# A hyperbolic-attention and fp8 layer: a new way to the first attention step, in one block

## The reference

```
arg    = max(1 + 2c |q - k|^2 / max((1 - c|q|^2)(1 - c|k|^2), EPS), 1 + EPS)
scores = -softplus(beta) * arccosh(arg) / sqrt(c) - attention_bias
w      = softmax(scores);   out = w @ log_map(v);   x1 = x + log_map(exp_map(out)) @ W_o^T
out    = x1 + bf16(fp8(LayerNorm(x1)) @ fp8(W_ffn) * scales) + bias
```

## Time and profile before

| | us |
|---|---|
| median of 3 runs | 2226.95 |
| lowest, highest | 2209.66, 2231.99 |
| the profiled execution's own time | 2226.39 |
| its span, first to last instruction | 2224.1 |

### The profile page before, as it was taken

One profiled execution on the slowest core, in us unless ns is written; L12 is line 12 of the kernel. 1 busy time (PEld: TensorE's weight loads), 2 busy tenths in 40 slices (PEclk: granted clock), 3 DMA queues, 4 the chain that ended last, 5 costly groups with the idle time before them and its releaser, 6 DMA issues. The chain is left out here.

```text
span 2224.1 us, 29561 instructions
## 1 busy us (share of the span) xinstructions
PE 1855.3 (83%) x10721; PEld 617.0 (28%) x10721; DVE 1172.3 (53%) x2869; ACT 1896.5 (85%) x1055; POOL 2.6 (0%) x15
## 2 busy tenths in 40 slices
PE   4459898998989859898989789898989898899792
PEld 2222222232322213222222222222222223233221
DVE  5563345555555545556555655555565555423335
ACT  1019999989999949999999699999999999999790
POOL 0000000000000000000000000000000000000000
PEclk9969999989999969999999899999999999999895
DMA  1031220313131211312213031312213031311000
GB/s 40 22 111 48 80 69 20 120 39 120 39 101 39 99 40 39 103 37 91 67 56 103 19 120 39 101 39 91 67 39 115 25 110 39 110 39 58 20 20 30
DMA packets 112937, 142.54 MB, mean 64 GB/s; under 512 B 35676, under 2 KB 61533, under 8 KB 112733
## 3 DMA queue, kind: packets, MB, share of 16 engines
q1 hardware_dynamic: 112732, 140.13, 20.1%
HBM read 85.07 MB, written 55.05 MB: 63 GB/s over the span
## 5 line engine op out<-in xcount | busy, mean ns | idle before, releaser
L888 ACT ACTIVATE U<-U,sc 128x2048 f32<-128x2048 f32 x512 | 1047.6, 2048 | 0.3
L881 ACT ACTIVATE U<-ps 128x2048 f32<-128x2048 f32 x500 | 959.8, 1920 | 63.6 <-PE ps L797 57.7
L797 PE MATMUL ps<-q_T,k_T 18*128 18x512 f32 x4096 | 638.8, 655 | 183.3 <-ACT U L881 132.7
L810 PE MATMUL ps<-U,vals 128*32 128x512 f32 x4096 | 564.9, 624 | 50.3 <-ACT U L888 42.6
L797 PEld LDWEIGHTS ps<-q_T,k_T 18*128 18x128 f32 x4096 | 200.4, 188 | 406.5 <-ACT U L881 318.1
L347 PE MATMUL ps<-wT,xnT 128*128 128x384 f32 x512 | 247.8, 574 | 17.1 <-DVE qkv L373 14.3
L373 DVE COPY qkv<-ps 128x384 f32<-128x384 f32 x128 | 71.3, 557 | 260.0 <-PE ps L347 259.9
L833 PE MATMUL ps<-woT,ident 128*128 128x256 f32 x428 | 157.9, 452 | 0.0
L956 DVE COPY OTs<-ps 128x512 f32<-128x512 f32 x64 | 44.3, 692 | 194.9 <-PE ps L810 173.4
L352 PE MATMUL ps<-ident,rows 128*128 128x128 f32 x512 | 110.3, 315 | 44.1 <-DVE rows L482 29.8
L347 PEld LDWEIGHTS ps<-wT,xnT 128*128 128x128 f32 x512 | 83.9, 202 | 222.9 <-issue 119.7
(11 more groups left out here) (164 smaller groups left out, 1168.9 us busy)
## 6 DMA issues: line engine op xcount, KB each, us to landing
rqb<-q_scratch SPq DMA_DIRECT2D x64, 1024.0 KB, 5.6
q_scratch<-q_T SPq DMA_DIRECT2D x16, 1024.0 KB, 4.5
k_scratch<-k_T SPq DMA_DIRECT2D x16, 1024.0 KB, 6.8
v_scratch<-vals SPq DMA_DIRECT2D x16, 768.0 KB, 9.2
xt<-in_L_attn_x_dram SPq DMA_DIRECT2D x16, 512.0 KB, 6.2
fi_xt<-in_L_attn_x_dram SPq DMA_DIRECT2D x16, 512.0 KB, 5.7
out_dram<-fi_x SPq DMA_DIRECT2D x16, 512.0 KB, 4.1
rk_scratch<-rk SPq DMA_DIRECT2D x16, 32.0 KB, 11.9
```

Of the source, the lines that this page charges most:

```text
L797: ins = pe.matmul(g.ps[:, 2 * pair + i, :], a.k_T[HB * h:HB * h + RD, b % 2, hg, kt * P:(kt + 1) * P], a.q_T[HB * h:HB * h + RD, G % 3, hg ...
L810: ins = pe.matmul(g.ps[HB * h:HB * h + VW, 6, :], a.vals[:, b % 2, kt, (hg * HPG + h) // 2, DH * (h % 2):DH * (h % 2) + VW], U[:, n % RING ...
L881: act.activation(U[:, n % RING].rearrange("p b n -> p (b n)"), chunk(n), ACT.Ln, scale=-2.0 / EPS, bias=1.0).then_inc(freed, 1)
L888: act.activation(U[:, n % RING], U[:, n % RING], ACT.Exp, scale=g.NEGB).then_inc(exp_done, 1)
```

## The change

The setup is no longer a block: `setup_stage` gives its pieces to the one block that is left, with its scratch in tiles that are used later (U, xb, sq and ocT of the finish stage). Every engine's order up to the first steps is written anew:

- SP issues x of group 0 first, then the weights, the scalars, x of group 1 (into the finish stage's xt), the FFN weight, and x of group 2.
- VectorE normalises group 0, computes the constants, normalises group 1, and then does each group's roots and rows (`first_vector`). Squares are done by ScalarE (`first_scalar`), sums by VectorE. The FFN weight is quantised in step 12.
- GpSimd clears and marks rows and vals (`pool_zero`).
- TensorE fills X, M and R of groups 0 and 1 in the order FIRST_FILLS, through banks 2 to 7; ScalarE empties them. The rows of k are formed and turned before those of q. A uses of group 0 have banks 0 and 1.
- distances(0) follow after R4 and R0 of group 0. The six other R of group 0 are filled after distances(1, 0), and copied by ScalarE in step 0. The R and A uses of group 1 lie in steps 2 to 20 (FIRST_USES), group 2's projection is wholly in the steps, with its own table (SECOND_USES). Group 1's stores are at step 21.

In the steps: the Exp's scale is a register, loaded once from g.NEGB; the small exponential e is in slot 20 instead of 19; on the open branch bound(n + 1) and clamp(n + 1) stand ahead of the copies of step n; copy_sums stands behind the copies of both halves; steps 0 to 2 hold no fillers.

```diff
+FIRST_USES = {("R", 4): (2, 0), ("A", 0): (2, 0), ("A", 1): (2, 1), ("R", 5): (3, BOTH), ("R", 6): (6, BOTH),
+              ("R", 7): (14, BOTH), ("R", 0): (16, BOTH), ("R", 1): (17, BOTH), ("R", 2): (19, BOTH),
+              ("R", 3): (20, BOTH)}
+SECOND_USES = dict(PROJECT_USES)
+SECOND_USES.update({("R", i): (24 + i, 0 if i in (3, 6) else BOTH) for i in range(8)})
+SECOND_USES.update({("A", 0): (27, 1), ("A", 1): (30, 1)})
+FIRST_FILLS = ([("X", 0, 0, 6), ("X", 0, 1, 7)] + [("M", 0, i, (2, 3, 4, 5, 6, 7, 2, 3)[i]) for i in range(8)]
+               + [("X", 1, 0, 4), ("X", 1, 1, 5)] + [("M", 1, i, (6, 7, 2, 3, 4, 5, 6, 7)[i]) for i in range(8)]
+               + [("R", 0, 4, 4), ("R", 0, 0, 5)]
+               + [("R", 0, i, bank) for i, bank in ((5, 6), (1, 7), (6, 6), (2, 7), (7, 6), (3, 7))])
...
+    def pool_zero(pool, setup):
+        step = Steps(pool, zeroed, 0)
+        step(pool.memset(rows[:, :, :, :, :], 0.0))
+        step(pool.memset(a.vals[:, :, :, :, DH:VW], 0.0))
+        step(pool.memset(rows[:, 0, :, :, 16:17], 1.0))
+        step(pool.memset(rows[:, 1, :, :, 17:18], -1.0))
+        setup.await_eab(pool)
+        for kt in range(KT):
+            for half in range(2):
+                ones = a.vals[half * 64:half * 64 + 64, :, kt, :, DH + 2 * kt + half]
+                step(pool.tensor_scalar(ones, ones, g.EAB[half * 64:half * 64 + 64], None, ALU.add))
...
+    def first_scalar(act, j):
+        kind, n, i, bank = FIRST_FILLS[j]
+        src = g.ps[:, bank, :]
+        act.wait_ge(p_filled, j + 1)
+        if kind == "X":
+            act.activation(xnT[:, i, :], src, ACT.Copy).then_inc(p_copied, 1)
+        elif kind == "M":
+            t, half = i // 2, i % 2
+            act.activation(qkv_of(n)[:, t, 24 * half:24 * (half + 1), :].rearrange("p h d -> p (h d)"),
+                           src[:, 0:384], ACT.Copy).then_inc(p_copied, 1)
+            if half == 1:
+                act.wait_ge(p_copied, j + 1)
+                if n == 1:
+                    act.wait_ge(reduced, t + 1)
+                act.activation(squares(t), qkv_of(n)[:, t].rearrange("p h d -> p (h d)"), ACT.Square).then_inc(squared, 1)
+        else:
+            qk, hg = i // HG, i % HG
+            dst = a.k_T[:, 0, hg, 0:GTOK] if qk else a.q_T[:, 0, hg, :]
+            act.activation(dst, src, ACT.Copy).then_inc(p_copied, 1)
...
     def scalar(act, n, k):
-        if k == 19:
+        if k == 20:
...
+                setup.scalar_weights(act)
+                first_copies("X", 0, range(2))
+                setup.scalar_constants(act)
+                first_copies("M", 0, range(8))
+                first_copies("X", 1, range(2))
+                first_copies("M", 1, range(2))
+                project.scalar(act, 0, 20)
+                first_copies("M", 1, range(2, 8))
+                setup.await_constants(act)
                 act.activation(past[:, :], g.NEGB, ACT.Exp, scale=math.log(2.0 * U_EXACT + 1.0)).then_inc(past_rdy, 1)
+                act.reg_load(exponent, g.NEGB[0:1, :].bitcast(I32))
+                first_copies("R", 0, (4, 0))
...
-                    act.activation(U[:, n % RING], U[:, n % RING], ACT.Exp, scale=g.NEGB).then_inc(exp_done, 1)
+                    act.activation(U[:, n % RING], U[:, n % RING], ACT.Exp, scale=exponent).then_inc(exp_done, 1)
...
+                        if not is_open and n == 0:
+                            other_copies()
+                        if not is_open and n == 1:
+                            project.scalar(act, 1, 20)
...
-                        if is_open:
-                            clamp(n)
-                            if n + 1 < n0 + UNIT:
-                                bound(n + 1)
+                        if is_open and n + 1 < n0 + UNIT:
+                            bound(n + 1)
+                            clamp(n + 1)
                         for key in in_step(G, s, 0):
                             copy(*key)
+                        for key in in_step(G, s, 1):
+                            copy(*key)
                         if n % KT == 0 and n >= KT:
                             copy_sums(n // KT - 1)
-                        for key in in_step(G, s, 1):
-                            copy(*key)
...
+                        if n == KERNEL_STEP:
+                            setup.vector_kernel(v)
...
+                for k in range(3):
+                    project.vector(v, 0, k, first)
+                setup.vector(v)
+                for k in range(3):
+                    project.vector(v, 1, k, first)
+                project.first_vector(v, 0, first)
+                for i in range(2):
+                    project.copy(v, 0, ("A", i))
+                project.first_vector(v, 1, first)
```

More of the change, by code:

```diff
@@ L366, in copy @@
         b, u = n // 2, n % 2
-        bank = g.ps[:, 7, :]
-        v.wait_ge(a.b7_filled, uses.after((kind, n, i)))
+        if n:
+            bank = g.ps[:, 7, :]
+            v.wait_ge(a.b7_filled, uses.after((kind, n, i)))
+        else:
+            bank = g.ps[:, i, :]
+            v.wait_ge(a_filled, i + 1)
         if kind == "X":
@@ L480, in vector @@
         if k == 23:
-            for qk in range(2):
+            for qk in (1, 0):
                 v.tensor_tensor(rows[:, qk, :, :, 0:DH], qkv[:, :, qk * H:(qk + 1) * H, :],
@@ L779, in _, with turned @@
                 sp.wait_ge(finish.stored, 16 * NG)
+            @block.gpsimd
+            def _(pool):
+                setup.pool_first(pool)
+                project.pool_zero(pool, setup)
             @block.tensor
             def _(pe):
+                def turned(n, i):
+                    if n == 0:
+                        pe.wait_ge(project.p_copied, FIRST_PLACE["R", n, i] + 1)
+                    else:
+                        pe.wait_ge(a.b7_copied, uses.after(("R", n, i)))
                 def distances(n, second):
@@ L871, in _, with first_copies, other_copies @@
                 act.preload_act_table_set(ACT_SET)
+                exponent = act.alloc_register("exponent")
+                def first_copies(kinds, n, numbers):
+                    for j, (kind, m, i, bank) in enumerate(FIRST_FILLS):
+                        if kind in kinds and m == n and i in numbers:
+                            project.first_scalar(act, j)
+                def other_copies():
+                    first_copies("R", 0, (1, 2, 3, 5, 6, 7))
                 def log(n, is_open):
@@ L924, in _ @@
             def _(v):
[L925 to L933 removed]
+                first = Steps(v, project.p_steps, 0)
+                first.mark(v.memset(ones_c[:, :], 1.0))
                 def bound(n):
@@ L1000, in unit @@
                             project.vector(v, m, k)
-                for k in range(LEAD):
-                    for half in range(2):
-                        for key in use_before_steps(k, half):
-                            copy(*key)
-                    for n, slot in before_steps(k):
-                        project.vector(v, n, slot)
+                        if n == KERNEL_STEP:
[9 more added lines that the diff above has]
+                project.first_vector(v, 1, first)
                 for n0 in range(0, N, UNIT):
```

450 lines of the change are left out of this document (260 added, 190 removed).

## The result

The changed kernel takes 2011.19 us (median of 4 runs, 2004.81 to 2014.07), the kernel before 2218.68 us beside it (4 runs, 2209.66 to 2231.99): a ratio of 0.9056 (0.8994 to 0.9119), 208 us less. The prediction of 2034.0 us is 23 us too high, and its range of 1995 to 2090 holds the time.

What follows compares the result with a forecast made beforehand. ScalarE was taken to bound the steps, with losses before the first step, at each projected group and on the open branch. Gains of 90 + 30 + 44 + 28 = 192 us from 2226.4 gave 2034 us, range 1995 to 2090.

Steps and rivals of the forecast that it cites:

- Part 1: Before the first step and in group 0: first Ln at 53 instead of 156 us; gain 90 us, bounds 70 to 98.
- two of them run at 2.93 us and six at 1.56 us: Group 0's eight M fills through six banks, without waiting for copies: two at half clock, six faster, ending at 31 us.
- at step 12 another 4 us of kernel quantisation: VectorE's quantisation before an M copy in group 0; with group 2's late normalisation, 6 us lost.
- Rival A: TensorE stays at half clock up to the first step: fourteen slower M fills, 19 us, so 2053 us; chance 0.15.
- Part 2: Exp's scale from a register saves 0.09 us each, 1.9 us a group, 30 us in all; bounds 0 to 60.
- Part 3: Small exponential one slot later: ScalarE's recurring wait for VectorE's nrm goes; gain 44 us, bounds 30 to 52.
- Part 4: Open branch: next step's bound and product go ahead of the bank-7 copy; gain 28 us, bounds 10 to 40.
- Part 5: The rest, including copy_sums behind its step's bank-7 copies: costed at nothing, or 20 us if the cover is gone.
- Rival C: TensorE, with VectorE's copies behind it, becomes the bound at 3.75 us an M step: 2077 us; chance 0.10.
- The rule on shared interfaces: GpSimd's tile clearing shares SBUF interfaces with VectorE, so VectorE's chain between 13 and 37 us would stretch; no size given.

Runs made afterwards that it cites:

- the yardstick: The changed kernel with no edit, run again as the reference of the experiments: 2010.25 us, ratio 0.9052 against the kernel before.
- the last experiment: Changed kernel with groups 1 and 2's uses kept out of group 0's steps 10 and 26, group 1's small exponential one step earlier: 2004.86 us, ratio 0.9025.

## Why the prediction was right, point by point

| part | forecast | measured | by |
|---|---|---|---|
| 1 way to the first step, group 0 included | 90 | 94.6; 81 to 99 | 107.5 - 12.9 in the two traces shown; between other pairs of executions |
| 2 register scale | 30 | 25 to 27 | alone in either kernel |
| 3 slot of e | 44 | 48 to 52; 51 | alone in the kernel before; groups 1 to 15 with it undone |
| 4 open branch | 28 | 40 | undone |
| 5 order of the sums | 0 | 6 to 8 | undone |
| whole | 192 | 208; 212; 221.1 | the medians; the medians beside the yardstick; the two spans shown |

Parts 2 to 5 close. Taken back one at a time, they lengthen groups 1 to 15 by 28.8, 50.9, 42.9 and 6.6 us in the traces, 129.2 in all, and between the kernel before and the changed kernel these groups differ by 125.7. Part 1 is weaker: it is only read off traces, no run had the old prologue with the new steps, and it depends on the execution. Up to the end of group 0 the three profiles with the old prologue take 271.5 to 285.6 us, and those of the changed kernel, of its second profile and of the experiment with the old open order 186.2 to 190.5: 81 to 99 us apart. The two executions shown are apart from their medians in opposite directions (2226.39 against 2218.68, 2004.81 against 2011.19), which is why 221.1 us lie between their spans and 208 between the medians. The forecast of 192 is 16 to 20 us below the medians, and these are the parts' own errors: parts 3 to 5 were sized some 25 us too small, part 2 some 4 too large. The luck is in part 1.

**Part 1** was right in the sum, as far as the executions let one tell, but from two errors that cancel. The first Ln came at 45.17 and not at 53. The step that failed is "two of them run at 2.93 us and six at 1.56 us": in this execution all eight ran fast, at 1.32 us each, and so shorter still than the 1.56 us of single fills with waits between them. M fills ended at 24.9 and not 31, nrm stood at 32.3 and not 37.5. Against it, the break before Ln(4) was larger than I had it: from Ln(0) to Ln(4) 26.1 us, where I had 23; that chain (copies, e of group 1, VectorE's second half, K rows, turn) was the right one, and the last experiment moved it. My other 6 us, "at step 12 another 4 us of kernel quantisation" and the late normalisation, had the right size and the wrong place: 6.2 us are lost in steps 10 and 26, where a second use meets the sums, and 2.6 us in step 4. That a moved table of uses puts new uses beside the sums can be read in the diff, and I didn't read it.

The granted clock can't decide at this place: it reads 1.00 up to 120 us in the kernel before, whose fills took 2.93 us from 35 to 64, and 1.00 in the changed kernel from 12 to 35 us, whose fills took 1.32. The durations tell the level. They are not the same in every execution: of ten profiles of kernels that keep this prologue, counting the moved clears and the single bank, five have the eight X products at 1.09 or 1.10 us and five at 1.97 us, and in the latter the first Ln of the unchanged prologue starts at 47.8 to 47.9 us, 2.7 us late. In these five the eight M fills take 12.8 to 13.1 us, so that the forecast's two slow fills are half right there (it had 15.3 us). Rival A, fourteen more slow fills, didn't come about in any. The prediction's remark that much of TensorE's busy time was at the half clock was too strong: the mean granted clock of the kernel before is 0.951, which is about a tenth of the span at the half clock, without the slow fills before the first step that this figure doesn't show.

**Part 2** was right in its mechanism: 1.9 us a group was forecast, 1.9 us measured in groups 1 to 13 of the changed kernel. The sum of 30 us is 3 to 5 us too large; group 0, where other waits rule, gave nothing visible.

**Part 3** was right in its mechanism, and 4 to 8 us small. With slot 20 alone, step 14 of groups 1 to 13 gave 40.7 us (38 forecast). Of the loss behind the stall I had counted 10 us out of 15; all of it went (14.9 us in steps 16 to 18). The W steps came to light and cost 6.6 us in step 15, where I had 4.

**Part 4** was right in its mechanism, and 12 us small. First to fourth Ln of the three units: forecast 21 us, 6 us saved, 14 us; measured 19.2, 7.1 saved (23.45 to 16.35), 13.3. That gives 33.9 us. What I left out are the steps behind the units: in group 5 the two distances of the Exps after them fell from 13.94 and 6.03 to 8.07 and 3.75 us.

**Part 5**: "I cost it at nothing" is the step that failed. The M copy that comes 0.6 us earlier was not hidden in the one step where it stands beside the sums, and that could be seen in the kernel before: 4.05 to 4.39 us among steps of 3.75.

**Rival C** was half there: M steps stay at 3.75 us and take 1 us a group from the register. The forecast had counted just that. **The rule on shared interfaces** did bite, by 2.3 us, of which all but the 0.24 us before the X fill were covered.

## What to carry to other kernels

Where an in-order engine waits for another for 2 us in a regular step, moving that one small instruction a step later can give back much more than the wait, since the next steps recover too; count everything up to the step at which the rhythm is even again. When a table of uses is moved, check each new place against what else the same engines do in that step, and look for steps a few tenths longer than their neighbours: they are where an order costs. A prologue is worth a timeline of its own, step by step with every engine, as it was nearly half of this gain. And where a clock has two levels, one profile of a prologue is one sample: here the first Exp came at 152.83 to 166.33 us with the same code before it, but for the small edits of the experiments.

## What the runs showed of the hardware that was not expected

A 4-element VectorE operation took 1.83 us instead of 0.17 while GpSimd cleared a tile, and ended 0.02 us after the clear. It is not every operation: the aggregate at 6.09 us, inside the same clear, took its usual 0.38 us. The Trainium skill, SBUF — State Buffer, section "SBUF: two separate sides", says that VectorE and GpSimd share a pair of ports as an exclusive lock, held for a whole instruction by whichever starts first, and that only some VectorE operations ask for it. The trace agrees, with 7.27 and 9.14 us as ends of the held operations beside 7.26 and 9.12 us of the clears.

The same code doesn't meet the same clock in every execution. In three profiles with the old prologue TensorE had been idle for 19.6 to 19.9 us, turned x, and began its M fills at 2.93 us. In two of them (the kernel before, and the register alone) all eight fills of group 0 stayed at 2.93 us, for 28 us, with 0.65 to 0.72 us of waiting before each; in the third (slot 20 alone) the second fill already took 1.56 us, and the granted clock reads 1.00 from 40 to 50 us. In the one-bank experiment one fill was slow after 2.46 us of idle time, and the next took 1.60 us. So it was neither the single bank nor the waits alone that held the clock down in the kernel before; what did, no run here shows. The Trainium skill, TensorE: Matmul & The Clock Gate, Part 1, says that the throttled state is the default and that activity releases it. The third profile and the one-bank experiment agree; the other two went 28 us of fills without a release.

An Exp of 2048 elements with its scale in a register is 0.09 us shorter than one with it in a tile (1961 against 2047 ns on average). In the open units of the changed kernel, where Ln reads SBUF too and has no operand in a tile, both take 1.91 us.
